# 64-row score products in pairs, the router's bias added by TensorE and its two largest read from PSUM, in a fused cross-attention and mixture-of-experts layer

## The chip, the cores and the metric

The kernel runs on one core of a Trainium2 chip. The metric is the device time of one execution in microseconds (us), and lower is better. The time shown for the kernel before is a median of three runs; the profile comes from one further execution, whose time stands beside its span below.

## The reference

What is computed, cut to what matters here (32 batches of 64 tokens, 128 features, 16 heads of 8 features, 16 experts of 64 hidden features, two experts for each token):

```python
qh, kh, vh = split_heads(layernorm(x), Wq), split_heads(ctx, Wk), split_heads(ctx, Wv)
scores = jnp.einsum('bhqd,bhkd->bhqk', qh, kh) / scale        # scale = dk ** -0.5
scores = jnp.where(mask, NEG_INF, scores)
attn = jax.nn.softmax(scores, axis=-1)
x = x + (einsum(attn, vh) joined over heads) @ Wo.T

flat = layernorm(x)
logits = flat @ router_w.T
topk_scores, topk_idx = jax.lax.top_k(logits + router_bias, 2)
topk_scores = jax.nn.softmax(topk_scores, axis=-1)            # weights of the two experts
hidden = silu(flat @ gate_e) * (flat @ up_e)                  # for each of the 16 experts
x = x + sum over experts of weight_e * (hidden @ down_e) + shared expert
```

## The kernel before, in words

Tokens are cut into 16 tiles of 128 (two batches of 64 each). The program has three stages. In the set-up, four groups of four tiles pass through `project` (lines 872 to 908): values, transposes of the normalised tokens, masked contexts, and then the queries and keys (line 903), whose heads of eight features end up on partitions. In the attention loop (`step`, lines 936 to 1003 on TensorE, with a `step` of the same numbering on each other engine) every round `t` works on several tiles at once: scores and softmax of tile `t+1`, transposes and values of tile `t`, the output projection of tile `t-1`, the second norm and the router of tile `t-2`, and on VectorE the two largest logits of tile `t-3`. In the last stage (`gate`, `up`, `down`, `slot`) the experts run as long chains of 512-column products.

Each engine has its instructions in a fixed, hand-written order and waits for semaphores that the others raise; nothing is reordered by a planner. An engine that waits holds up all that stands behind the wait.

TensorE's order in a round, as far as the change touches it: `scores(0)` (eight heads, one product over 128 rows with 512 columns, line 964); `values_as_rows` (914); four transposes of the first half of the probabilities (945); `scores(1)` (964 again, the other eight heads); `attention_transposed` (919, which waits for VectorE's attention result); four transposes of the second half (945); `norm_transposed` (930); `output_projection` (924); `values` (954, 16 small products on 32-column tiles of the array); `router` (934). A product in 32-bit floats shows in the trace as two matmul instructions.

The operands of a score product are built by GpSimd: `q_block` (418) spreads the queries so that the two batches do not mix, and `k_blocks` (426) makes, for each half of the heads, 512 columns of keys masked by head.

VectorE's order in a round: the residual add (705); the router's bias added to the logits (708); `bn_stats` (713); the largest eight (717); `bn_aggr` (721); their indices (725); the difference of the two largest (727); the negated mean (730); the indices as floats (733); `row_max(0)` (738); the reciprocal (747) and the product (749) that make the attention result of tile `t-1`; the subtraction of the maximum (759) for the first half; `row_max(1)` and the subtraction for the second half. ScalarE copies transposed probabilities (542, twice), normalises (554), copies the transposed attention result (558), copies the transposed norm twice (564, 565) and takes the exponentials (547).

From round 12 on VectorE has added work for the experts' weights (`top_two`, `two_weights`, `weigh_experts`), and from round 15 on TensorE's place for the scores is taken by the first expert products (1013).

Of the kernel before, what the change touches and what calls it, by code (L numbers as in the profile page):

```python
# [22 lines left out]
ROWS = HG * DK  # L23
# [17 lines left out]
def build_program(nc, x, ctx_nat, ctx_t, mask_row, mask_col, w_att, router_bias, w_moe, consts, out):  # L41
    stack = ExitStack()
    with stack:
# [7 lines left out]
        consts_sb = sb("consts_sb", [P, P + HG + 2 + EXPERTS])  # L51
        ident_sb = consts_sb[:, 0:P]
        hmask_sb = consts_sb[:, P:P + HG]
        half_mask_sb = consts_sb[:, P + HG:P + HG + 2]
        iota_sb = consts_sb[:, P + HG + 2:]
        bias_sb = sb("bias_sb", [P, EXPERTS])
        w_att_sb = sb("w_att_sb", [P, 4 * D + EXPERTS])
        wq_sb, wk_sb, wv_sb, wo_sb = (w_att_sb[:, i * D:(i + 1) * D] for i in range(4))
        wr_sb = w_att_sb[:, 4 * D:]
# [20 lines left out]
        half_sb = sb("half_sb", [P, P])  # L80
# [20 lines left out]
        k_blk = [sb(f"k_blk{p}", [P, 2, HG, S]) for p in range(2)]  # L101
# [10 lines left out]
        neg_mean2 = [sb(f"neg_mean2_{p}", [P, 1]) for p in range(2)]  # L112
# [5 lines left out]
        logit = [sb(f"logit{p}", [P, EXPERTS]) for p in range(2)]  # L118
        top_v = [sb(f"top_v{p}", [P, 8]) for p in range(2)]
        top_i = [sb(f"top_i{p}", [P, 8], U32) for p in range(2)]  # L120
# [78 lines left out]
        s_nmean2 = sem("s_nmean2")  # L199
# [8 lines left out]
        s_logit_sb = sem("s_logit_sb")  # L208
# [41 lines left out]
        up_ps = [banks[6], banks[0]]  # L250
        ct_ps = [banks[2][:, (2 + h) * P:(3 + h) * P] for h in range(2)]
# [133 lines left out]
        def _(pool):  # L385
            nc.gpsimd.memset(half_sb[:, :], 0.5).then_inc(s_half, 1)
# [27 lines left out]
            def q_block(t, p, first):  # L414
                if not first:
                    pool.wait_ge(s_score[1], t - 1)

                nc.gpsimd.tensor_tensor(
                    q_blk[p][:, :, :, :],
                    q_all[:, bass.ds(t, 1), :, :].rearrange("p o g (c s) -> p (o g) c s", c=1).broadcast_to([P, 2, BPT, S]),  # L420
                    half_mask_sb.rearrange("p (o b e) -> p o b e", o=1, e=1).broadcast_to([P, 2, BPT, S]), ALU.mult)

            def k_blocks(t, p):

                for g in range(2):
                    last = nc.gpsimd.tensor_tensor(  # L426
                        k_blk[p][:, g, :, :],
                        k_all[:, bass.ds(t, 1), g, :].broadcast_to([P, HG, S]),
                        hmask_sb.rearrange("p (h o) -> p h o", o=1).broadcast_to([P, HG, S]), ALU.mult)
                last.then_inc(s_blk, 1)  # L430
# [27 lines left out]
            def step(t, p, on):  # L458
                if on(-2):
                    q_block(t + 2, p, first=False)  # L460
                if on(2):
# [6 lines left out]
                    pool.wait_ge(s_nmean2, t - 1)  # L468
                    nc.gpsimd.tensor_tensor(bias2[p][:, :], neg_mean2[p][:, :], rstd2[p][:, :], ALU.mult).then_inc(s_bias2, 1)
# [19 lines left out]
        def _(act):  # L489
# [3 lines left out]
            act.dma_start(bias_sb[:, :], router_bias.broadcast_to([P, EXPERTS])).then_inc(s_wproj, 16)  # L493
# [82 lines left out]
            def tanh_of(half):  # L576

                tiles = slice(half * TILES // 2, (half + 1) * TILES // 2)
                act.wait_ge(s_top_f, (half + 1) * TILES // 2)
# [53 lines left out]
        def _(dve):  # L633
# [28 lines left out]
            nc.vector.tensor_scalar(n_valid[:, :], count_ps[:, 0:BATCHES], 1.0, None, ALU.max).then_inc(s_cnt, 1)  # L662
# [19 lines left out]
            def top_two(half):  # L682
# [4 lines left out]
                dve.wait_ge(s_top_f, (half + 1) * TILES // 2)  # L687
# [12 lines left out]
            def step(t, p, on):  # L700
# [13 lines left out]
                if on(3):  # L714
                    dve.wait_ge(s_logit_sb, t - 2)
                    nc.vector.memset(pause[:, q:q + 1], 0.0)
                    nc.vector.max(top_v[q][:, :], logit[q][:, :]).then_inc(s_top_v, 1)
# [4 lines left out]
                if on(3):  # L722
                    dve.wait_ge(s_top_v, t - 2)
                    nc.vector.memset(pause[:, 2 + q:3 + q], 0.0)
                    nc.vector.max_index(top_i[q][:, :], top_v[q][:, :], logit[q][:, :]).then_inc(s_top_i, 1)
                    tile = bass.ds(t - 3, 1)
                    nc.vector.tensor_tensor(gap[:, tile], top_v[q][:, 1:2], top_v[q][:, 0:1], ALU.subtract)
                if on(2):
                    dve.wait_ge(s_mv2, t - 1)
                    nc.vector.tensor_scalar(neg_mean2[p][:, :], mv2[p][:, 0:1], -1.0, None, ALU.mult).then_inc(s_nmean2, 1)  # L730
                if on(3):
                    dve.wait_ge(s_top_i, t - 2)
                    nc.vector.tensor_copy(top_f[:, tile, :].rearrange("p o k -> p (o k)"),
                                          top_i[q][:, 0:2]).then_inc(s_top_f, 1)
# [58 lines left out]
            dve.wait_ge(s_wproj, 32)  # L793
# [64 lines left out]
        def _(pe):  # L858
            def keep_busy(products):

                for _ in range(products):
                    nc.tensor.matmul(score_ps[0][:, 0:P], half_sb[:, :], half_sb[:, :], start=True, stop=True)
# [4 lines left out]
            nc.tensor.matmul(count_ps[:, 0:BATCHES], half_sb[:, :], valid_key[:, :], start=True,  # L867
# [4 lines left out]
            def project(g, p, first=False):  # L872
                if first:
                    pe.wait_ge(s_wproj, 32)
# [21 lines left out]
                for w, src, have, dst, drained, made in ((wq_sb, xt_sb, s_xt_sb, q_ps, s_q_sb, s_q),  # L896
# [4 lines left out]
                    for hg in range(2):  # L901
# [244 lines left out]
```

## Time and profile before

| | before |
|---|---|
| median of three runs | 193.76 us (193.52 to 194.12) |
| the profiled execution, its own time | 194.68 us |
| its span, first to last instruction | 192.9 us |
| mean granted TensorE clock | 0.976 of full speed |
| busy: TensorE, VectorE, ScalarE, GpSimd | 179.3, 168.8, 124.6, 92.1 us |
| score products, line 964 | 64 instructions, 34.0 us busy |
| key blocks, line 426 | 32 instructions, 32.7 us busy |

The page is read as follows. "Busy" of TensorE is the union of its matmuls, whose ends are modelled and reach about 0.16 us past the moment at which the next one may start; two starts therefore tell more than a duration. Weight loads (PEld) run beside the matmuls. A group "x2" in a timeline is two instructions merged into one row. An idle time in brackets names what ended it.

### The profile page before, as it was taken

To read this page: it belongs to the slowest core of one execution; us is meant where nothing else is said; L and a number is where in the kernel's file an instruction comes from. 1 tells how busy PE (TensorE), PEld (TensorE's weight loads), DVE (VectorE), ACT (ScalarE), POOL (GpSimd) and SP (SyncE) were. 2 spreads that over 40 slices of the span, in tenths; PEclk is the share of its full clock that TensorE was granted. 3 is DMA by queue.
4 is the path that set the end of the run, shared out by engine and by line. 5 is a ranking of instruction groups with operands and counts; after the bars stand their busy time and mean duration, and the time that the engine had idled before them with its cause. 6 is when DMAs were issued, how large, how long until landed. Compare 5 with 4: busy or idle time off the path is not lost.

```text
span 192.9 us, 4173 instructions
## 1 busy us (share of the span) xinstructions
PE 179.3 (93%) x1351; PEld 131.8 (68%) x1351; DVE 168.8 (87%) x515; ACT 124.6 (65%) x280; POOL 92.1 (48%) x148
## 2 busy tenths in 40 slices
PE   7599599999999999999998799999999999999962
PEld 7497467566666666666666466778888888888841
DVE  6899999589999999989995799988899889988981
ACT  2168374777888888888885855466655665565641
POOL 5746992758988988888786690300000000000000
PEclk9969979999999999999999999999999999999997
DMA  5984910000000000000000174332363236324401
GB/s 135 286 249 92 352 40 0 5 0 0 3 2 5 0 3 0 3 0 2 5 0 3 57 198 139 110 110 82 128 180 115 72 126 171 120 82 126 120 0 54
DMA packets 13202, 15.33 MB, mean 79 GB/s; under 512 B 1665, under 2 KB 8193, under 8 KB 13057
## 3 DMA queue, kind: packets, MB, share of 16 engines
q1 hardware_dynamic: 12608, 14.57, 24.8%
q10 hardware_dynamic: 576, 0.55, 1.2%
q8 instruction: 9, 0.15, 0.3%
q14 instruction: 9, 0.07, 0.1%
HBM read 13.93 MB, written 1.18 MB: 78 GB/s over the span
## 4 chain that ended last, share of the span: by engine, by line
PE 61%; DVE 19%; ACT 5%; issue 5%; POOL 0%; DVEq 0%; POOLq 0%
PE bank L1013 26%; PE bank L964 12%; PE bank L945 5%; PE bank L954 5%; DVE hid L823 2%; PE bank L903 2%; ACT hid_hi L598 2%; PE bank L934 2%; DVE prob L759 2%; PE bank L924 2%; DVE smax L738 2%; DVE xn L649 2%; DVE hid_lo L815 2%; DVE cmix_sb L823 2%; PE bank L893 1%
## 5 line engine op out<-in xcount | busy, mean ns | idle before, releaser
L589 ACT ACTIVATE sig<-bank 128x512 f32<-128x512 f32 x36 | 21.5, 600 | 21.0 <-PE bank L1013 20.4
L964 PE MATMUL bank<-k_blk,q_blk 128*128 128x512 f32 x64 | 34.0, 615 | 0.0
L426 POOL TENSOR_TENSOR k_blk<-k_all,consts_sb 128x512 f32<-128x512 f32 x32 | 32.7, 1045 | 0.0
L1013 PE MATMUL bank<-xt_hi,w_hi 128*128 (+1 forms) x72 | 29.1, 405 | 0.0
L1013 PE MATMUL bank<-xt_lo,w_hi 128*128 (+1 forms) x72 | 28.4, 394 | 0.0
L1013 PE MATMUL bank<-xt_hi,w_lo 128*128 (+1 forms) x72 | 28.3, 393 | 0.0
L542 ACT COPY prob_t<-bank 128x512 f32<-128x512 f32 x32 | 18.8, 586 | 11.5 <-PE bank L945 11.5
L806 DVE TENSOR_TENSOR hid_u<-sig,bank 128x512 f32<-128x512 f32 x32 | 21.9, 684 | 4.2 <-PE bank L1013 2.5
L738 DVE TENSOR_REDUCE smax<-bank 128x8 f32<-128x512 f32 x32 | 21.9, 686 | 2.6 <-PE bank L964 2.6
L759 DVE TENSOR_TENSOR prob<-bank,smax 128x512 f32<-128x512 f32 x32 | 22.0, 687 | 0.6
L547 ACT ACTIVATE prob<-prob 128x512 f32<-128x512 f32 x32 | 20.8, 653 | 0.0
L945 PE MATMUL bank<-consts_sb,prob 128*128 128x128 f32 x128 | 19.2, 273 | 0.0
L598 ACT CAST hid_hi<-hid 128x512 fp32r<-128x512 f32 x24 | 14.9, 621 | 6.4 <-DVE hid L823 6.4
L815 DVE TENSOR_TENSOR hid_lo<-hid,hid_hi 128x512 fp32r<-128x512 f32 x24 | 16.7, 697 | 1.7 <-ACT hid_hi L598 1.0
L1013 PE MATMUL bank<-hid_hi,w_hi 128*128 128x512 f32 (+1 forms) x37 | 15.1, 409 | 2.2 <-DVE hid_lo L815 2.2
L945 PEld LDWEIGHTS bank<-consts_sb,prob 128*128 128x128 f32 x128 | 15.1, 141 | 1.1 <-issue 1.1
L1013 PEld LDWEIGHTS bank<-xt_hi,w_lo 128*128 128x128 f32 x72 | 13.5, 188 | 3.0
L1013 PEld LDWEIGHTS bank<-xt_hi,w_hi 128*128 128x128 f32 x72 | 13.6, 189 | 2.8
L1013 PEld LDWEIGHTS bank<-xt_lo,w_hi 128*128 128x128 f32 x72 | 13.6, 188 | 2.7
L1013 PE MATMUL bank<-hid_hi,w_lo 128*128 128x512 f32 (+1 forms) x37 | 14.4, 390 | 0.0
L1013 PE MATMUL bank<-hid_lo,w_hi 128*128 128x512 f32 (+1 forms) x37 | 14.4, 388 | 0.0
L823 DVE TENSOR_TENSOR hid<-hid_u,mix_all 128x512 f32<-128x512 f32 x20 | 13.9, 697 | 0.0
(116 smaller groups left out, 378.8 us busy)
## 6 DMA issues: line engine op xcount, KB each, us to landing
mix_all<-w_rows SPq DMA_DIRECT2D x64, 128.0 KB, 2.9
w_moe_sb<-w_moe SPq DMA_DIRECT2D x1, 1728.0 KB, 9.9
x_sb<-x SPq DMA_DIRECT2D x4, 256.0 KB, 7.6
ctxt_sb<-ctx_t SPq DMA_DIRECT2D x4, 256.0 KB, 5.9
ctx_sb<-ctx_nat SPq DMA_DIRECT2D x4, 256.0 KB, 5.1
out<-x_sb SPq DMA_DIRECT2D x3, 256.0 KB, 2.3
w_att_sb<-w_att ACTq DMA_DIRECT2D x1, 264.0 KB, 5.8
mrow<-mask_row ACTq DMA_DIRECT2D x1, 256.0 KB, 4.9
```

Of the source, the lines that this page charges most:

```text
L426: last = nc.gpsimd.tensor_tensor(k_blk[p][:, g, :, :], k_all[:, bass.ds(t, 1), g, :].broadcast_to([P, HG, S]), hmask_sb.rearrange("p (h o) ...
L542: nc.scalar.copy(prob_t[p][:, h * GT:(h + 1) * GT, :], pt_ps[h][:, :].rearrange("p (j q) -> p j q", q=P)).then_inc(s_pt_sb[h], 1)
L547: nc.scalar.activation(prob[q][:, g * GN:(g + 1) * GN], prob[q][:, g * GN:(g + 1) * GN], ACT.Exp, scale=SCORE_SCALE).then_inc(s_exp[g], 1)
L589: nc.scalar.activation(sig[r][:, :], gate_ps[r][:, :], ACT.Silu).then_inc(s_sig, 1)
L738: nc.vector.tensor_reduce(smax[q][:, g * HG:(g + 1) * HG], score_ps[g][:, :].rearrange("p (h s) -> p h s", s=S), AX_X, ALU.max).then_inc(s ...
L759: nc.vector.tensor_tensor(prob[q][:, g * GN:(g + 1) * GN].rearrange("p (h s) -> p h s", s=S), score_ps[g][:, :].rearrange("p (h s) -> p h ...
L806: nc.vector.tensor_tensor(dst[:, :], sig[r][:, :], up_ps[r][:, :], ALU.mult).then_inc(s_hid_u, 1)
L815: nc.vector.tensor_tensor(hid_lo[k][:, cols], hid[k][:, cols], hid_hi[k][:, cols].bitcast(F32), ALU.subtract).then_inc(s_hid_lo, 1)
L823: nc.vector.tensor_tensor(hid[m % 3][:, :], hid_u[r][:, :], spread[k], ALU.mult).then_inc(s_hid, 1)
L945: last = nc.tensor.transpose(pt_ps[h][:, j * P:(j + 1) * P], prob[p][:, c:c + P], ident_sb)
L964: nc.tensor.matmul(score_ps[g][:, :], q_blk[q][:, g, :, :].rearrange("p b s -> p (b s)"), k_blk[q][:, g, :, :].rearrange("p h s -> p (h s) ...
L1013: last = nc.tensor.matmul(out, w, moving, start=start and k == 0, stop=stop and k == 2)
```

## The change

The score product of eight heads over 128 rows and 512 columns becomes two products of four heads each, over 64 rows and 256 columns. The rows of the two head groups lie on different halves of the array (rows 0 to 63 and 64 to 127), and their results in different PSUM banks, so a product of one group stands next to one of the other. All four products stand at the head of the round, and the second group's wait for VectorE's subtraction stands there too. The query and key projections write eight pieces of 32 partitions instead of four of 64. GpSimd builds the keys of a tile in one instruction of 512 columns instead of two.

The router's bias is now a product of its own (a matrix of ones by a row of biases) that accumulates with the logits, in columns of a PSUM bank of their own. VectorE takes the largest eight and their indices straight from PSUM. The difference of the two largest and the conversion of the indices are done once for four tiles. The negated mean is gone (GpSimd multiplies by -1 in the instruction that makes the norm's bias). The transposed norm now waits for the indices of the tile before it, where it waited for the biased logits. The DMA that spread the router's bias over the partitions is gone; the biases come with the attention weights. The matrix of halves in the set-up is one of ones, and the count is halved by VectorE.

```diff
 def k_blocks(t, p):
-    for g in range(2):
-        last = nc.gpsimd.tensor_tensor(k_blk[p][:, g, :, :], ...)
-    last.then_inc(s_blk, 1)
+    nc.gpsimd.tensor_tensor(k_blk[p][:, :, :, :], ...).then_inc(s_blk, 1)
...
-                    pool.wait_ge(s_nmean2, t - 1)
-                    nc.gpsimd.tensor_tensor(bias2[p][:, :], neg_mean2[p][:, :], rstd2[p][:, :], ALU.mult).then_inc(s_bias2, 1)
+                    nc.gpsimd.tensor_scalar(bias2[p][:, :], mv2[p][:, 0:1], rstd2[p][:, :], -1.0, ALU.mult,
+                                            ALU.mult).then_inc(s_bias2, 1)
...
-            act.dma_start(bias_sb[:, :], router_bias.broadcast_to([P, EXPERTS])).then_inc(s_wproj, 16)
...
                 if on(3):
                     dve.wait_ge(s_logit, t - 2)
-                    nc.vector.tensor_tensor(logit[q][:, :], tail_ps[:, 0:EXPERTS], bias_sb[:, :],
-                                            ALU.add).then_inc(s_logit_sb, 1)
+                    nc.vector.max(top_v[:, t - 3, :], logit_ps).then_inc(s_top_v, 1)
                 if on(2):
                     (bn_stats)
                 if on(3):
-                    dve.wait_ge(s_logit_sb, t - 2)
-                    nc.vector.max(top_v[q][:, :], logit[q][:, :]).then_inc(s_top_v, 1)
+                    dve.wait_ge(s_top_v, t - 2)
+                    nc.vector.max_index(top_i[:, t - 3, :], top_v[:, t - 3, :], logit_ps).then_inc(s_top_i, 1)
                 if on(2):
                     (bn_aggr)
-                if on(3):
-                    dve.wait_ge(s_top_v, t - 2)
-                    nc.vector.max_index(top_i[q][:, :], top_v[q][:, :], logit[q][:, :]).then_inc(s_top_i, 1)
-                    nc.vector.tensor_tensor(gap[:, tile], top_v[q][:, 1:2], top_v[q][:, 0:1], ALU.subtract)
-                if on(2):
-                    nc.vector.tensor_scalar(neg_mean2[p][:, :], mv2[p][:, 0:1], -1.0, None, ALU.mult).then_inc(s_nmean2, 1)
-                if on(3):
+                if on(3) and (t - 2) % GT == 0:
+                    nc.vector.tensor_tensor(gap[:, tiles], top_v[:, tiles, 1], top_v[:, tiles, 0], ALU.subtract)
                     dve.wait_ge(s_top_i, t - 2)
-                    nc.vector.tensor_copy(top_f[:, tile, :]..., top_i[q][:, 0:2]).then_inc(s_top_f, 1)
+                    nc.vector.tensor_copy(top_f[:, tiles, :], top_i[:, tiles, 0:2]).then_inc(s_top_f, 1)
...
-                    for hg in range(2):
-                        for b in range(BPT):
-                            last = nc.tensor.matmul(
-                                dst[b * ROWS:(b + 1) * ROWS, hg * GT * S:(hg + 1) * GT * S], ...)
+                    for j in range(2):
+                        for hg in range(2):
+                            for b in range(BPT):
+                                row, head = hg * ROWS + b * QROWS, hg * HG + j * HQ
+                                last = nc.tensor.matmul(
+                                    dst[row:row + QROWS, j * GT * S:(j + 1) * GT * S], w[:, head * DK:(head + HQ) * DK],
+                                    ..., start=True, stop=True, tile_position=(0, row))
...
             def norm_transposed(t, p):
-                    pe.wait_ge(s_logit_sb, t)
+                    pe.wait_ge(s_top_i, t)
             def router(t, p):
                 pe.wait_ge(s_xt2_hi, t + 1)
-                nc.tensor.matmul(tail_ps[:, 0:EXPERTS], xt2[p][:, :], wr_sb, start=True, stop=True).then_inc(s_logit, 1)
+                nc.tensor.matmul(logit_ps, ones_sb[:, :], bias_row_sb, start=True, stop=False)
+                nc.tensor.matmul(logit_ps, xt2[p][:, :], wr_sb, start=False, stop=True).then_inc(s_logit, 1)
...
-                def scores(g):
-                    if not (once and t < 0):
-                        pe.wait_ge(s_sub[g], t + 1)
-                    nc.tensor.matmul(score_ps[g][:, :], q_blk[q][:, g, :, :]..., k_blk[q][:, g, :, :]...,
-                                     start=True, stop=True).then_inc(s_score[g], 1)
+                def scores():
+                    for j in range(2):
+                        for g in range(2):
+                            if j == 0 and not (once and t < 0):
+                                pe.wait_ge(s_sub[g], t + 1)
+                            rows = slice(g * ROWS, (g + 1) * ROWS)
+                            last = nc.tensor.matmul(score_ps[g][:, j * HQ * S:(j + 1) * HQ * S],
+                                                    q_blk[q][rows, j, :, :]..., k_blk[q][rows, j, :, :]...,
+                                                    start=True, stop=True, tile_position=(g * ROWS, 0))
+                            if j == 1:
+                                last.then_inc(s_score[g], 1)
                 if on(-1):
                     pe.wait_ge(s_blk, t + 2)
-                    scores(0)
+                    scores()
...
                 if on(0):
                     transposes(0)
-                if on(-1):
-                    scores(1)
-                else:
+                if not on(-1):
```

## Rows read from the trace of the kernel before

**Rows 1.** Busy time by stretch: window, length, busy time of each engine, granted clock.
```profile
56.00:64.00 8.00, 8.00 (x102) 5.36 (x100) 7.65 (x35) 6.56 (x19) 7.03 (x14) 1.00 0.01 3
```

**Rows 2.** Timeline of TensorE (start us, us, engine, line): starts of rounds 2, 13, 15.
```profile
41.91 0.70 PE L964 MATMUL bank<-k_blk,q_blk 128*128 128x512 f32 x1
...
90.98 0.68 PE L964 MATMUL bank<-k_blk,q_blk 128*128 128x512 f32 x1
...
100.28 0.48 PE L1013 MATMUL bank<-xt_hi,w_hi 128*128 128x512 f32 x1
```

**Rows 3.** Timeline of TensorE in round 6.
```profile
59.77 1.10 PE L964 MATMUL bank<-k_blk,q_blk 128*128 128x512 f32 x2
60.71 0.38 PE L914 MATMUL bank<-consts_sb,pvt_sb 128*128 128x128 f32 x2
60.93 0.60 PE L945 MATMUL bank<-consts_sb,prob 128*128 128x128 f32 x4
61.37 1.02 PE L964 MATMUL bank<-k_blk,q_blk 128*128 128x512 f32 x2
62.23 0.27 PE L919 MATMUL bank<-consts_sb,att 128*128 128x128 f32 x1
62.34 0.60 PE L945 MATMUL bank<-consts_sb,prob 128*128 128x128 f32 x4
...
63.27 0.78 PE L954 MATMUL bank<-prob_t,v_all 128*18 128x64 f32 x32
63.98 0.40 PE L934 MATMUL bank<-w_att_sb,xt 128*128 128x16 f32 x2
```

**Rows 4.** Timeline of VectorE in the same round.
```profile
60.65 0.14 DVE L727 TENSOR_TENSOR gap<-top_v 128x1 f32<-128x1 f32 x1
...
60.91 0.69 DVE L738 TENSOR_REDUCE smax<-bank 128x8 f32<-128x512 f32 x1
...
61.80 0.29 DVE L749 TENSOR_TENSOR att<-bank,inv_den 128x128 f32<-128x128 f32 x1
...
63.32 0.69 DVE L759 TENSOR_TENSOR prob<-bank,smax 128x512 f32<-128x512 f32 x1
...
64.42 0.17 DVE L708 TENSOR_TENSOR logit<-bank,bias_sb 128x16 f32<-128x16 f32 x1 [0.21 <-PE bank L934]
```

**Rows 5.** Timeline of ScalarE in the same round.
```profile
61.57 0.59 ACT L542 COPY prob_t<-bank 128x512 f32<-128x512 f32 x1 [0.55 <-PE bank L945]
...
62.54 0.27 ACT L558 COPY att_t<-bank 128x128 f32<-128x128 f32 x1
62.97 0.59 ACT L542 COPY prob_t<-bank 128x512 f32<-128x512 f32 x1 [0.17 <-PE bank L945]
...
63.61 0.28 ACT L565 CAST xt_hi<-bank 128x128 fp32r<-128x128 f32 x1
```

**Rows 6.** Timeline of TensorE in the set-up; first row: a window of 0.05 us.
```profile
31.89 0.44 PE L903 MATMUL bank<-xt_sb,w_att_sb 128*64 128x256 f32 x2
...
31.89 1.08 PE L903 MATMUL bank<-xt_sb,w_att_sb 128*64 128x256 f32 x8
32.81 1.03 PE L903 MATMUL bank<-cmix_sb,w_att_sb 128*64 128x256 f32 x8
33.77 0.70 PE L964 MATMUL bank<-k_blk,q_blk 128*128 128x512 f32 x1
...
27.76 1.98 PE L964 MATMUL bank<-k_blk,q_blk 128*128 128x512 f32 x4
29.58 0.27 PE L879 MATMUL bank<-w_att_sb,ctxt_sb 128*128 128x128 f32 x1
```

**Rows 7.** Timelines of VectorE and TensorE where VectorE is late, rounds 13 and 15.
```profile
93.34 0.29 DVE L749 TENSOR_TENSOR att<-bank,inv_den 128x128 f32<-128x128 f32 x1
...
93.86 0.27 PE L945 MATMUL bank<-consts_sb,prob 128*128 128x128 f32 x1
...
103.38 0.33 PE L919 MATMUL bank<-consts_sb,att 128*128 128x128 f32 x1 [0.80 <-DVE att L749]
```

More of the change, by code:

```diff
@@ L22 @@
 HG = HEADS // 2
-ROWS = HG * DK
+HQ = HG // 2
+QROWS = HQ * DK
+ROWS = BPT * QROWS
 PAIRS = HEADS // 2
@@ L38, with build_program @@
 SCORE_SCALE = float(DK) ** 0.5
-def build_program(nc, x, ctx_nat, ctx_t, mask_row, mask_col, w_att, router_bias, w_moe, consts, out):
+def build_program(nc, x, ctx_nat, ctx_t, mask_row, mask_col, w_att, w_moe, consts, out):
     stack = ExitStack()
@@ L48, in sem @@
             return stack.enter_context(nc.semaphore(name))
-        consts_sb = sb("consts_sb", [P, P + HG + 2 + EXPERTS])
+        consts_sb = sb("consts_sb", [P, P + HQ + 2 * BPT + EXPERTS])
         ident_sb = consts_sb[:, 0:P]
[L53 to L57, printed above, removed]
+        hmask_sb = consts_sb[:, P:P + HQ]
+        half_mask_sb = consts_sb[:, P + HQ:P + HQ + BPT]
+        batch_mask_sb = consts_sb[:, P + HQ + BPT:P + HQ + 2 * BPT]
+        iota_sb = consts_sb[:, P + HQ + 2 * BPT:]
+        w_att_sb = sb("w_att_sb", [P, 4 * D + 2 * EXPERTS])
         wq_sb, wk_sb, wv_sb, wo_sb = (w_att_sb[:, i * D:(i + 1) * D] for i in range(4))
-        wr_sb = w_att_sb[:, 4 * D:]
+        wr_sb, bias_row_sb = (w_att_sb[:, 4 * D + i * EXPERTS:4 * D + (i + 1) * EXPERTS] for i in range(2))
         w_moe_sb = sb("w_moe_sb", [P, W_MOE])
@@ L100, in build_program @@
         q_blk = [sb(f"q_blk{p}", [P, 2, BPT, S]) for p in range(2)]
-        k_blk = [sb(f"k_blk{p}", [P, 2, HG, S]) for p in range(2)]
+        k_blk = [sb(f"k_blk{p}", [P, 2, HQ, S]) for p in range(2)]
         pvt_sb = sb("pvt_sb", [P, 2 * P])
@@ L116, in build_program @@
         xt2 = [sb(f"xt2_{p}", [P, P]) for p in range(2)]
-        logit = [sb(f"logit{p}", [P, EXPERTS]) for p in range(2)]
-        top_v = [sb(f"top_v{p}", [P, 8]) for p in range(2)]
-        top_i = [sb(f"top_i{p}", [P, 8], U32) for p in range(2)]
+        top_v = sb("top_v", [P, TILES, 8])
+        top_i = sb("top_i", [P, TILES, 8], U32)
         top_f = sb("top_f", [P, TILES, 2])
@@ L861, in keep_busy @@
                 for _ in range(products):
-                    nc.tensor.matmul(score_ps[0][:, 0:P], half_sb[:, :], half_sb[:, :], start=True, stop=True)
+                    nc.tensor.matmul(score_ps[0][:, 0:P], ones_sb[:, :], ones_sb[:, :], start=True, stop=True)
             pe.wait_ge(s_half, 1)
@@ L866, in _ @@
             pe.wait_ge(s_valid, 1)
-            nc.tensor.matmul(count_ps[:, 0:BATCHES], half_sb[:, :], valid_key[:, :], start=True,
+            nc.tensor.matmul(count_ps[:, 0:BATCHES], ones_sb[:, :], valid_key[:, :], start=True,
                              stop=True).then_inc(s_nvalid, 1)
@@ L900, in project @@
                         pe.wait_ge(drained, g)
[L901 to L907 removed]
+                    for j in range(2):
[4 more added lines that the diff above has]
+                                    dst[row:row + QROWS, j * GT * S:(j + 1) * GT * S], w[:, head * DK:(head + HQ) * DK],
+                                    src[p][:, :].rearrange("p (t b s) -> p t b s", b=BPT, s=S)[:, :, b, :],
+                                    start=True, stop=True, tile_position=(0, row))
                     last.then_inc(made, 1)
@@ L1118, in host_layout @@
     w_moe = np.stack([gate, up, down], axis=2).reshape(P, W_MOE)
-    w_att = np.concatenate([a["L0_xattn_" + w].T for w in ("Wq", "Wk", "Wv", "Wo")] + [a["L0_ffn_router_w"].T], axis=1)
+    bias_row = np.zeros((P, EXPERTS), np.float32)
+    bias_row[0] = a["L0_ffn_router_bias"].reshape(EXPERTS)
+    w_att = np.concatenate([a["L0_xattn_" + w].T for w in ("Wq", "Wk", "Wv", "Wo")] + [a["L0_ffn_router_w"].T, bias_row], axis=1)
     ident = np.eye(P, dtype=np.float32)
-    head_of_row = (np.arange(P) % ROWS) // DK
-    head_mask = (head_of_row[:, None] == np.arange(HG)[None, :]).astype(np.float32)
+    row = np.arange(P)
+    head_mask = (row[:, None] % QROWS // DK == np.arange(HQ)[None, :]).astype(np.float32)
+    batch_mask = (row[:, None] % ROWS // QROWS == np.arange(BPT)[None, :]).astype(np.float32)
     half_mask = (np.arange(P)[:, None] // S == np.arange(2)[None, :]).astype(np.float32)
```

49 lines of the change are left out of this document (19 added, 30 removed).

## The prediction

> **What bounds the kernel now.** I read the busy time by stretch first. In the attention loop all engines look full: TensorE is busy for 8.00 of 8.00 us, VectorE 7.65, GpSimd 7.03, ScalarE 6.56, at full clock [rows 1]. By that view a change that takes work from TensorE, VectorE and GpSimd at once must win. But a busy TensorE is not a TensorE that streams, so the next view is the timeline of one round, read for what each start waits on. Round 2 begins at 41.91 and round 13 at 90.98 [rows 2]: 11 rounds of 4.46 us. One closed path has that length. The first score product starts at 59.77 [rows 3]; VectorE's first row maximum, which needs it, starts 1.14 later at 60.91; the reciprocal and the attention product follow in VectorE's order and end at 61.80 + 0.29 = 62.09, 1.18 later [rows 4]. TensorE's line 919 waits for that, and the second four transposes start at 62.34, 0.25 later [rows 3]. ScalarE copies them from 62.97, 0.63 later, after an idle 0.17 that TensorE ends, and its last copy ends at 63.61 + 0.28 [rows 5]. The router starts at 63.98, 1.01 after 62.97, and the next scores 0.25 after that [rows 3]. 1.14 + 1.18 + 0.25 + 0.63 + 1.01 + 0.25 = 4.46. The reader is to see that the second score product is on this path only as a tie: it starts at 61.37 and takes 62.23 - 61.37 = 0.86, and line 919 starts at its end [rows 3], 0.14 after the attention result, which had to be signalled in any case.
>
> **The change part by part.**
>
> *Score products.* Each is two instructions; 512 columns take 0.86, so 256 columns take 0.215 for one instruction. No 64-row product stands in the trace; the nearest are the query and key projections, which sit on two halves of the array by columns. There two instructions start within 0.05 us, and eight of 256 columns take 32.81 - 31.89 = 0.92 and 33.77 - 32.81 = 0.96 [rows 6], where 8 x 0.215 = 1.72 would be one after another. So I take pairs as overlapping: four products are eight instructions in four slots, 0.86, plus 0.10 for weights that could not be loaded ahead (0.94 - 0.86 = 0.08 of that is paid before, between 59.77 and 60.71 [rows 3]), and 0.20 until VectorE starts, as before (60.91 - 60.71). That is 1.16 against 1.14: the pair is done when one product was done before. What is saved is 0.86 of TensorE a round in the middle, and there line 919 waits for VectorE instead. Where VectorE is late already, the second four start 93.86 - (93.34 + 0.29) = 0.23 after the attention result [rows 7] against 0.25: the gain on the path is 0.02.
>
> *Going in and out of tiles.* In the 0.96 above, 0.10 is more than four slots: leaving column tiles for the whole array costs 0.10 [rows 6]. I take the same for entering 64-row tiles after the router, on the path; between 0 and 0.20 (the two transitions around line 954 are no dearer) are its ends. Leaving them again costs as much, beside VectorE's row maximum.
>
> The Trainium skill, "TensorEngine Tiling (Array Packing)", Tiling Modes, Key Properties, says that a change of tiling mode (not of tile) drains the engine. The 0.10 agrees with it; without it the sum would be 0.10 a round lower.
>
> *The router's bias.* Two instructions of 16 columns by 128 rows more, behind the same wait for the copied norm. Four instructions that each load 128 columns take 61.37 - 60.93 = 0.44 [rows 3], and the router's own two hold the next score for 0.25, so two more cost 0.22 (between 0 and 0.25), at the one point of the round where TensorE goes straight on to the next scores.
>
> *New path.* 0.10 + 1.16 + 1.18 + 0.23 + 0.63 + 1.01 + (0.25 + 0.22) = 4.78. A second branch comes level: both scores now end before the first transposes, so the first copy of probabilities starts at 0.10 + 0.10 + 0.86 + 0.10 + 0.22 + 0.44 + 0.06 (weights not loaded ahead) + 0.20 = 2.08 after the router (before: 1.80 [rows 3, 5]); the copy of the attention result stands 0.97 behind it in ScalarE's order, and from there to the router it is 1.44 less 0.10 in which line 954 waits [rows 3, 5]: 4.39, with the router 4.86. So 4.82, 0.36 a round more.
>
> *Work taken off that lies beside the path.* GpSimd loses one of two key blocks, VectorE four small instructions (60.91 - 60.65 = 0.26 for three of them [rows 4], and the logits' add). VectorE idles for 0.21 in every round until the router is done [rows 4]; its shed work makes that idle longer. The moved wait of the second group for the subtraction is covered: VectorE needs 63.32 + 0.69 - 60.91 = 3.10 from the first row maximum to the end of the last subtraction [rows 4], so that ends at 1.26 + 3.10 = 4.36, 0.4 before TensorE gets there; if that cover went, values, transposes and all behind the scores would stand still for VectorE. The wait of the transposed norm for the indices is covered by some 2 us of other work. The projections in four column tiles cost the same if four overlap: line 954 has 32 instructions on such tiles within 63.98 - 63.27 = 0.71 [rows 3], 0.022 each where 64 columns alone would take 0.054. The DMA taken off feeds the first projection, which stands well ahead of what VectorE lets through; 0, with 1 us either way for the clock in the set-up.
>
> *Ends of the loop.* The four instructions of the first tile's scores take 29.58 - 27.76 = 1.82 [rows 6] on a TensorE with nothing between; they become 0.10 + 0.86 + 0.10 = 1.06 and a little for weights, -0.7. Rounds 0 and 1 have no router and follow VectorE: +0.1. Rounds 13 and 14 together took 100.28 - 90.98 = 9.30 [rows 2], held by VectorE's added work, which now fits: 2 x 4.82 - 9.30 = +0.34. Behind them, VectorE's shed 0.3 shortens an idle of 0.80 [rows 7], and three routers with bias add up to 0.6: +0.1.
>
> *Sum.* -0.7 + 0.1 + 11 x 0.36 + 0.34 + 0.1 = +3.8. Against the profiled execution, 194.68 (span 192.9 and 1.8 around it): 198.5. The median is 0.92 below that execution, so I expect 193.76 + 3.8 = 197.6.
>
> **The rivals.**
>
> *VectorE's round (faster).* If TensorE's streaming is what sets 4.46, as its 8.00 of 8.00 says, then 0.86 off and 0.32 on would bring it under VectorE's own round: 3.10 + 0.05 + 0.96 + 0.20 = 4.31. That is 11 x -0.15, -0.7 at the start, -0.5 in rounds 13 and 14 and -0.2 behind: -3.1, 190.7. It decides if the path from the attention result to the next scores shrinks by 0.5. Against it speaks VectorE's idle 0.21 before the logits in each round, ended by the router [rows 4].
>
> *Pairs that overlap in part.* If the second pass of a product must wait for its first and holds up its neighbour, eight instructions take five slots. The first group ends as above, the second 0.22 later, and the second branch grows to 5.08: 11 x 0.62 and about 0.3 in all else, 200.9. The Trainium skill, "TensorE: Matmul & The Clock Gate", Part 3, What overlaps and what doesn't, has matmuls start and end strictly in order; taken with two passes behind each other it gives this case. The two starts within 0.05 us [rows 6] speak against it.
>
> *No overlap.* Eight slots: the second branch grows by 0.86 to 5.7, about +17: 211. Nothing in the trace shows row tiles; that is all that speaks for it.
>
> *Nothing to be measured.* If the entry is free and the bias hides in the router's wait, a round costs 0.02 to 0.1 more, which the 0.7 at the start pays: 193.2 to 194.3.
>
> **How the numbers follow.** Forecast (0.2 to 0.45 a round, 195.7 to 198.9) 0.55, partial overlap 0.10, none 0.05, nothing 0.12, VectorE's round or another gain 0.18. A difference of 0.3% is about what a measurement of this kernel can tell from none. Faster 0.18, same 0.12, slower 0.70. The range, 191.8 to 201.2, leaves out no overlap and most of the faster case.
>
> **What would show it.** Right: rounds of 4.75 to 4.9; line 919 (in its new place) with idle time ended by the attention product; four instructions for the router, some 0.47 to the next scores; VectorE idle for 0.5 or more a round, GpSimd at some 60%. The score instructions start in pairs, four slots of 0.215; starts 0.215 apart one by one would mean no overlap. Wrong: a round of 4.3 with VectorE without idle time; a round whose scores wait for the subtraction; a clock below full in the loop.

## The result, and the profile after

| | before | after |
|---|---|---|
| median of the runs made side by side | 193.82 us (193.52 to 194.12) | 196.97 us (196.84 to 197.16) |
| ratio, 95% interval | | 1.015 (1.0112 to 1.0188) |
| profiled execution, its span | 194.68, 192.9 us | 197.0, 195.2 us |
| busy: TensorE, VectorE, ScalarE, GpSimd | 179.3, 168.8, 124.6, 92.1 us | 175.2, 164.5, 123.1, 76.8 us |
| score products | 34.0 us busy | 18.9 us busy |
| key blocks | 32.7 us busy | 16.6 us busy |

Every engine has less to do and the kernel is 3.15 us slower. The busy time by stretch (window, length, busy time of TensorE, its weight loads, VectorE, ScalarE, GpSimd, then the granted clock) answers [rows 1]: no engine is full any more.

```profile
56.00:64.00 8.00, 7.08 (x106) 5.56 (x106) 7.20 (x24) 6.00 (x17) 5.00 (x10) 1.00 0.01 2
```

TensorE's timeline of after (start us, duration us, engine, line, operation, tiles, shapes, count; in brackets the idle time before and what ended it) gives the starts of rounds 2 and 13 and of the first expert product, which answer [rows 2]; then round 6, for [rows 3]; then the set-up, for [rows 6]. Line 956 is the score products, 902 the values as rows, 907 the transposed attention result, 934 the transposes of probabilities, 922 the bias and 923 the router; 866 is the work of the set-up that follows the first tile's scores.

```profile
40.46 0.48 PE L956 MATMUL bank<-k_blk,q_blk 64*128 64x256 f32 x1
...
92.91 0.49 PE L956 MATMUL bank<-k_blk,q_blk 64*128 64x256 f32 x2
...
102.35 0.49 PE L1006 MATMUL bank<-xt_hi,w_hi 128*128 128x512 f32 x1
...
59.57 1.13 PE L956 MATMUL bank<-k_blk,q_blk 64*128 64x256 f32 x8
60.64 0.44 PE L902 MATMUL bank<-consts_sb,pvt_sb 128*128 128x128 f32 x2
...
61.97 0.33 PE L907 MATMUL bank<-consts_sb,att 128*128 128x128 f32 x1 [0.46 <-DVE att L737]
62.14 0.60 PE L934 MATMUL bank<-consts_sb,prob 128*128 128x128 f32 x4
...
63.79 0.39 PE L922 MATMUL bank<-w_att_sb,ones_sb 128*128 128x16 f32 x2
64.03 0.37 PE L923 MATMUL bank<-w_att_sb,xt 128*128 128x16 f32 x2
64.33 0.49 PE L956 MATMUL bank<-k_blk,q_blk 64*128 64x256 f32 x2
...
25.93 1.14 PE L956 MATMUL bank<-k_blk,q_blk 64*128 64x256 f32 x8
27.00 1.16 PE L866 MATMUL bank<-w_att_sb,ctxt_sb 128*128 128x128 f32 x8
...
32.52 0.70 PE L956 MATMUL bank<-k_blk,q_blk 64*128 64x256 f32 x4
```

VectorE and ScalarE in the same round, for [rows 4, 5] (line 726 is the row maximum, 737 the attention product, 705 the largest eight; 539 copies transposed probabilities, 551 normalises, 555 copies the transposed attention result):

```profile
60.74 0.69 DVE L726 TENSOR_REDUCE smax<-bank 128x8 f32<-128x512 f32 x1 [0.26 <-PE bank L956]
...
61.63 0.29 DVE L737 TENSOR_TENSOR att<-bank,inv_den 128x128 f32<-128x128 f32 x1
...
64.44 0.18 DVE L705 MAX8 top_v<-bank 128x8 f32<-128x16 f32 x1 [0.41 <-PE bank L923]
```
```profile
61.55 0.59 ACT L539 COPY prob_t<-bank 128x512 f32<-128x512 f32 x1 [1.03 <-PE bank L934]
62.03 0.50 ACT L551 ACTIVATE xn<-x_sb,bias,rstd 128x128 f32<-128x128 f32 x1
62.43 0.25 ACT L555 COPY att_t<-bank 128x128 f32<-128x128 f32 x1
62.77 0.59 ACT L539 COPY prob_t<-bank 128x512 f32<-128x512 f32 x1
```

A round lasts (92.91 - 40.46) / 11 = 4.77 where it lasted 4.46. The eight score instructions are done in 60.64 - 59.57 = 1.07, where one after another they would take 8 x 0.215 = 1.72. They start in four pairs, at 59.57, 59.89, 60.11 and 60.32, the two of a pair 6 to 7 ns apart. What they freed shows as the idle 0.46 ahead of line 907, which waits for VectorE as before. From the router to the next scores it is 64.33 - 63.79 = 0.54 where it was 0.25 [rows 3]. Nearly all of the 0.31 that a round has lost lies there.

### The profile page after: what moved, and what is told of

Same layout as the page of the kernel before. It is cut to its first block, busy times and chain, and to the rows that moved or that the text cites. A ratio compares the mean times of both kernels' runs of the same rounds, so it can differ in the third digit from the quotient of the medians.

```text
span 195.2 us, 4387 instructions
## 1 busy us (share of the span) xinstructions
PE 175.2 (90%) x1511; PEld 135.0 (69%) x1511; DVE 164.5 (84%) x443; ACT 123.1 (63%) x280; POOL 76.8 (39%) x132
## 3 DMA queue, kind: packets, MB, share of 16 engines
HBM read 13.93 MB, written 1.18 MB: 77 GB/s over the span
## 4 chain that ended last, share of the span: by engine, by line
PE 55%; DVE 20%; issue 5%; ACT 3%; DMA 3%; POOL 1%; DVEq 0%; SPq 0%
PE bank L1006 26%; PE bank L956 9%; PE bank L943 5%; DVE smax L726 5%; PE bank L934 3%; DVE hid L810 2%; PE bank L912 2%; PE bank L907 2%; PE bank L922 2%; DVE att L737 2%; ACT hid_hi L595 2%; DVE xn L646 2%; DVE cmix_sb L810 2%; DMA mix_all<-w_rows 2%; PE bank L923 1%
## 5 line engine op out<-in xcount | busy, mean ns | idle before, releaser
L539 ACT COPY prob_t<-bank 128x512 f32<-128x512 f32 x32 | 18.7, 587 | 16.6 <-PE bank L934 15.5
L956 PE MATMUL bank<-k_blk,q_blk 64*128 64x256 f32 x128 | 18.9, 403 | 0.0
L424 POOL TENSOR_TENSOR k_blk<-k_all,consts_sb 128x512 f32<-128x512 f32 x16 | 16.6, 1040 | 0.0
```

What stands on the lines that cost most here:

```text
L539: nc.scalar.copy(prob_t[p][:, h * GT:(h + 1) * GT, :], pt_ps[h][:, :].rearrange("p (j q) -> p j q", q=P)).then_inc(s_pt_sb[h], 1)
L956: last = nc.tensor.matmul(score_ps[g][:, j * HQ * S:(j + 1) * HQ * S], q_blk[q][rows, j, :, :].rearrange("p b s -> p (b s)"), k_blk[q][row ...
```

## The experiments

All edits are shown against the changed kernel, but for the last two, and cut to what matters. Each ratio is to the kernel before, run in the same set; its median there was 194.2 to 194.7 us, above the 193.82 of the result, so the ratios tell more than the times.

*Each half of the change alone.* First the pairs alone: score products, projections and key blocks as in the changed kernel; router, bias, largest two, indices and negated mean as in the kernel before.

```diff
-nc.tensor.matmul(logit_ps, ones_sb[:, :], bias_row_sb, start=True, stop=False)
-nc.tensor.matmul(logit_ps, xt2[p][:, :], wr_sb, start=False, stop=True)
+nc.tensor.matmul(tail_ps[:, 0:EXPERTS], xt2[p][:, :], wr_sb, start=True, stop=True)
...
-nc.vector.max(top_v[:, t - 3, :], logit_ps)
+nc.vector.tensor_tensor(logit[q][:, :], tail_ps[:, 0:EXPERTS], bias_sb[:, :], ALU.add)
```

> The kernel before with the score products in pairs alone (64 rows, 256 columns, all four at the head of the round, key blocks in one instruction, projections in 32-partition pieces); the router, its bias and VectorE's small instructions as before. My theory, the closed path scores, row maximum, attention product, second transposes, copies, router: a round grows by the entry into 64-row tiles (0.08) and 0.03 more until the row maximum, less 0.03 at line 919, so 4.54 us against 4.46, and the start of the loop gains about 0.6; in all 193.5 to 194.5. Rival, TensorE's streaming sets the round: 0.86 of TensorE's work goes, VectorE's round of 4.3 remains, about 191.

Then the router's part alone, with two score products over 128 rows in their old places:

```diff
-scores()
+scores(0)
...
 transposes(0)
+scores(1)
```

> The kernel before with the router's part alone (bias as a product, largest two from PSUM, difference and indices per four tiles, no DMA of the bias); scores, projections and key blocks as before. My theory: the two instructions of the bias product stand on the path, 4.46 + 0.22 = 4.68 us a round, while the start of the loop comes about 1.2 earlier for want of the DMA; 195 to 196. Rival, the work taken off VectorE counts: rounds of 4.2 to 4.3, under 192. Rival, the bias product hides behind the wait for the copied norm: 4.46, about 192.5.

And the whole change with the bias added by VectorE again:

```diff
-nc.tensor.matmul(logit_ps, ones_sb[:, :], bias_row_sb, start=True, stop=False)
+nc.vector.tensor_tensor(logit[q][:, :], logit_ps, bias_sb[:, :], ALU.add)
```

> The changed kernel with one part undone: the router's bias is added by VectorE again (one instruction from PSUM into SBUF, the largest and their indices from there), the bias by a DMA of its own that TensorE does not wait for; the rest as changed. My theory: the round falls from 4.76 to 4.54 us and the time by 11 to 13 rounds of 0.22 and a little at the end, 194 to 194.7. Rival, the bias product costs nothing: 4.76 and 197; if VectorE's instructions count, a little more than that.

Measured: pairs alone 194.91 us, ratio 1.0029 (1.0008 to 1.005); router alone 197.14, 1.015 (1.0112 to 1.0189); bias by VectorE 194.6, 1.0015 (0.9995 to 1.0036). TensorE's timelines of the three, starts of rounds 2 and 13:

```profile
41.07 0.48 PE L970 MATMUL bank<-k_blk,q_blk 64*128 64x256 f32 x1
...
91.07 0.49 PE L970 MATMUL bank<-k_blk,q_blk 64*128 64x256 f32 x2
```
```profile
41.84 0.70 PE L950 MATMUL bank<-k_blk,q_blk 128*128 128x512 f32 x1
...
93.38 0.68 PE L950 MATMUL bank<-k_blk,q_blk 128*128 128x512 f32 x1
```
```profile
40.76 0.48 PE L965 MATMUL bank<-k_blk,q_blk 64*128 64x256 f32 x1
...
90.76 0.49 PE L965 MATMUL bank<-k_blk,q_blk 64*128 64x256 f32 x2
```

Rounds of 50.00 / 11 = 4.55, 51.54 / 11 = 4.69 and 4.55. So the pairs cost 0.08 a round and the bias product 0.22 to 0.23, and the two add up to the whole change, 0.31. The rival that TensorE's streaming sets the round falls with the pairs alone: the score products held TensorE for 1.07 a round instead of 0.94 + 0.86, and the round grew. Nothing else in the change touches the round: the third kernel keeps the conversions for four tiles and goes without the negated mean, and its round is that of the pairs alone. The rounds came as expected, the times not quite. The pairs alone took 0.4 more than the upper end, which is what the kernel before took more in this set (194.21 us). The router alone took 1.1 more, since it did not begin its rounds 1.2 earlier for want of one DMA (round 0 at 33.70 against 33.77 [rows 6]). The DMA is worth nothing that shows.

*Is the router's place the cause?* If scores wait for router and bias, moving these off that place should free the round until VectorE sets it. Here the router of tile t-3 runs right behind the scores, and VectorE reads its logits at the end of its round (rounds 3 to 14):

```diff
 scores()
+router(t - 3, q)
...
-router(t - 2, p)
```

> The changed kernel with the router of tile t-3 behind the scores of round t instead of the router of tile t-2 ahead of the scores of round t+1 (rounds 3 to 14), and VectorE's reading of its logits at the end of its round. My theory: the router is the last piece of the closed path, and without it TensorE's scores wait for VectorE's last subtraction, a round of 4.3 to 4.35 us, VectorE with no idle time beyond its wait for the scores; 191 to 192.5. Rival, something else than the wait in front of the router sets the round: 4.76 stays, 197.

196.5 us, 1.0104 (1.0069 to 1.0138): from round 3 on the round is 4.62 to 4.66, not 4.3 to 4.35. TensorE's timeline of one round, then ScalarE's:

```profile
73.12 1.14 PE L971 MATMUL bank<-k_blk,q_blk 64*128 64x256 f32 x8
74.18 0.40 PE L937 MATMUL bank<-w_att_sb,ones_sb 128*128 128x16 f32 x2
...
74.90 0.60 PE L949 MATMUL bank<-consts_sb,prob 128*128 128x128 f32 x4
...
77.14 0.67 PE L958 MATMUL bank<-prob_t,v_all 128*18 128x64 f32 x32
77.74 0.49 PE L971 MATMUL bank<-k_blk,q_blk 64*128 64x256 f32 x2
```
```profile
75.53 0.59 ACT L539 COPY prob_t<-bank 128x512 f32<-128x512 f32 x1 [1.08 <-PE bank L949]
...
76.41 0.25 ACT L555 COPY att_t<-bank 128x128 f32<-128x128 f32 x1
```

The router now stands ahead of the first transposes, so ScalarE's first copy starts 75.53 - 73.12 = 2.41 behind the scores (after: 61.55 - 59.57 = 1.98), its normalising and its copy of the attention result, 0.88 later, come as late, and the values, which stand behind the transposed norm and the output projection made from these, start at +4.02 (after: 63.15 - 59.57 = 3.58). The branch through ScalarE that the prediction had named took the path over. The two rounds with a conversion for four tiles last as long (4.65 and 4.64) by another path: there VectorE's conversion takes 0.54 and the row maximum waits for VectorE. Rounds 13 and 14, 4.90 and 5.56, give back 1.0 of what the others gain against after. The router has to stand in a place where TensorE idles, and after has one, the 0.46 ahead of line 907. So the same kernel with the router behind the first four transposes:

```diff
 transposes(0)
+router(t - 3, q)
 attention_transposed(t - 1, q)
```

> The changed kernel, with the router products of tile t-3 (not t-2) run in round t for rounds 3 to 14, placed behind the first four transposes of the probabilities, where TensorE idles some 0.46 us until the attention product is ready. Theory: what holds the changed kernel's round at 4.76 is that the next score product stands behind router and bias; with these 0.45 us in an idle place, and off the path behind the last sums, the closed path is VectorE's own round, 3.10 of work and a gap of 1.22 for the score product: 4.32 a round, 12 rounds, 191 to 193 us, faster than both kernels. Rival: as in the run with the router directly behind the scores, ScalarE's queue (second copy of transposed probabilities, norm, attention copy) closes the path: 4.55 to 4.65 a round, 195 to 196.5 us.

And, since the idle place exists only because of the pairs, the same move with whole score products, the router behind the second:

```diff
-scores()
+scores(0)
...
 transposes(0)
+scores(1)
+router(t - 3, q)
 attention_transposed(t - 1, q)
```

> Unpaired scores of 128 rows, as in the kernel before, with the changed router and bias, the router products of tile t-3 run in round t behind the second half of the scores. Theory: the two halves of the scores fill TensorE up to the transposes, so that the moved products delay the transposes or the attention product's transposes; 4.5 to 4.7 a round, 194.5 to 197 us, no better than the kernel before. Rival: if only the router's place mattered and not the pairs, the round would be VectorE's, 4.3 to 4.4, and the time 191 to 193.5 us.

With pairs: 194.09 us, 0.9978 (0.9952 to 1.0004). Without: 198.29 us, 1.0198 (1.0159 to 1.0236). With pairs, TensorE in round 6, then VectorE in rounds 7 and 8 and the busy time from 58 to 72:

```profile
58.46 1.23 PE L971 MATMUL bank<-k_blk,q_blk 64*128 64x256 f32 x8
...
60.33 0.29 PE L937 MATMUL bank<-w_att_sb,ones_sb 128*128 128x16 f32 x2
...
60.86 0.33 PE L920 MATMUL bank<-consts_sb,att 128*128 128x128 f32 x1
...
62.73 0.53 PE L971 MATMUL bank<-k_blk,q_blk 64*128 64x256 f32 x2
```
```profile
63.08 0.15 DVE L722 TENSOR_TENSOR gap<-top_v 128x4 f32<-128x4 f32 x1
63.20 0.53 DVE L724 CAST top_f<-top_i 128x8 f32<-128x8 uint32 x1
...
66.77 0.69 DVE L752 TENSOR_TENSOR prob<-bank,smax 128x512 f32<-128x512 f32 x1
...
68.65 0.69 DVE L731 TENSOR_REDUCE smax<-bank 128x8 f32<-128x512 f32 x1
```
```profile
58.00:72.00 14.00, 13.38 (x208) 10.80 (x204) 13.34 (x51) 11.74 (x34) 9.44 (x19) 1.00 0.01 3
```

A round lasts 62.73 - 58.46 = 4.27 (4.22 to 4.28 in nine of the twelve from round 2 on), and VectorE goes from one instruction to the next with no wait over some 0.05 us (busy 13.34 of 14.00): its last subtraction ends at 66.77 + 0.69 = 67.46, the scores of round 8 start at 67.48, and the row maximum at 68.65, where VectorE has only just done its small instructions. The round is VectorE's, as the theory had it. The time missed its 191 to 193. What lies on VectorE is now on the path: the two rounds with a conversion for four tiles (0.15 + 0.53) took 4.75 and 4.80, and rounds 13 and 14, with VectorE's first work for the experts' weights, 5.06 and 5.30 (after: 4.76 and 4.68). And this execution's round 2 began late, at 41.47. Without pairs TensorE's timeline shows the moved products pushing line 917 behind them:

```profile
61.10 1.02 PE L965 MATMUL bank<-k_blk,q_blk 128*128 128x512 f32 x2
61.97 0.29 PE L934 MATMUL bank<-w_att_sb,ones_sb 128*128 128x16 f32 x2
...
62.33 0.31 PE L917 MATMUL bank<-consts_sb,att 128*128 128x128 f32 x1
```

There the round stays at 4.63, and at 5.1 where four tiles are converted; with rounds 13 and 14 of 5.36 and 5.71 the time is over the 194.5 to 197 expected. So, with the bias as a product, pairs and place are worth something only together: the pairs make room in the middle of the round, and something on the path has to be moved into it. Not run is the router in the idle place with the bias added by VectorE; the addition (0.17 [rows 4]) would then lie on the engine that sets the round.

*How do pairs form?* The changed kernel with the instructions of the upper 64 rows queued first, then those of the lower:

```diff
-for j in range(2):
-    for g in range(2):
+for g in range(2):
+    for j in range(2):
```

> The changed kernel with the eight score instructions of a round queued group by group: the four that use the upper 64 rows first, then the four that use the lower 64, so that only the middle two neighbours are on different halves. Theory: two instructions overlap only where neighbours in the queue use different halves: about seven slots of 0.216 in place of four, some 0.65 us more a round, 5.3 to 5.5 a round, 204 to 208 us. Rival: the halves run on their own whatever the order: 4.76 a round as in the changed kernel, 197 us.

A single execution, 198.14 us. Its timeline of TensorE: a window of 0.1 us, then the eight, then what follows them.

```profile
60.29 0.49 PE L956 MATMUL bank<-k_blk,q_blk 64*128 64x256 f32 x2
...
60.29 1.14 PE L956 MATMUL bank<-k_blk,q_blk 64*128 64x256 f32 x8
61.36 0.33 PE L902 MATMUL bank<-consts_sb,pvt_sb 128*128 128x128 f32 x1
```

Two start at once (13 ns apart) and the eight take 61.36 - 60.29 = 1.07, as in after; the rounds last 4.76. The theory of neighbours falls: the order within the score products does not matter. In the trace the second of the two carries the wait for VectorE's subtraction of the second group, so it belongs to the lower rows, and TensorE started it ahead of three instructions of the upper rows that were queued before it. The execution is 1.2 us longer than the median of after, of which the set-up holds 0.7: rounds 0 and 13 start 0.70 and 0.72 later than in after (33.22 and 93.63), with a granted clock of 0.59 from 24 to 28.

*The version the runs point to.* The kernel with the router in the idle place, with the indices of four tiles converted by ScalarE one round later, where it waits for the first transposes:

```diff
+act.wait_ge(s_top_i, t - 3)
+nc.scalar.copy(top_f[:, tiles, :], top_i[:, tiles, 0:2]).then_inc(s_top_f, 1)
...
+nc.vector.tensor_tensor(gap[:, tiles], top_v[:, tiles, 1], top_v[:, tiles, 0], ALU.subtract)
 nc.vector.max_index(top_i[:, t - 3, :], top_v[:, t - 3, :], logit_ps).then_inc(s_top_i, 1)
-four_tiles()
```

(`four_tiles` is the same difference and VectorE's conversion, so the edit also moves the difference ahead of the search for the indices.)

> The kernel with the router products in TensorE's idle place, whose rounds took 4.22 to 4.28 us with VectorE busy without a gap, and 4.75 to 4.80 where four tiles' indices were converted (conversion 0.53, difference 0.15); here ScalarE converts the indices of four tiles, one round later, ahead of its first copy of transposed probabilities, where it idled 0.58. Theory: VectorE's work is what the round lasts now, so the three longer rounds fall to 4.40 and the time by 3 x 0.4 = 1.2 to 1.5 us against that kernel, to a ratio of 0.989 to 0.993 to the kernel before, some 192.5 us. Rival: ScalarE's queue, which holds the second copy, the norm and the attention copy, closes the path as soon as anything is added to it: no gain, ratio 0.996 to 1.0.

193.05 us, 0.9951 (0.9922 to 0.998): between theory and rival in time, with the theory's rounds (4.22 to 4.37, from the start of round 2 to that of 13; the two with a conversion before, 4.32 and 4.37). Its timelines of VectorE, GpSimd and TensorE show one loss at the loop's end (line 769 is the difference, 453 GpSimd's splitting of expert weights, 943 the bias, 1029 the first expert product):

```profile
97.12 0.98 DVE L769 TENSOR_TENSOR gap<-top_v 128x4 f32<-128x4 f32 x1
...
95.17 2.92 POOL L453 TENSOR_TENSOR w_lo<-w_moe_sb,w_hi 128x384 fp32r<-128x384 f32 x3
...
98.42 0.36 PE L943 MATMUL bank<-w_att_sb,ones_sb 128*128 128x16 f32 x2 [1.39 <-DVE top_i L770]
...
98.85 0.48 PE L1029 MATMUL bank<-xt_hi,w_hi 128*128 128x512 f32 x1
```

TensorE's bias product waits for the index search, and that now stands behind a difference of 0.98: round 14 took 6.20, where the kernel without this edit took 5.30. So the edit made this loss itself, by moving the difference (why it takes so long beside GpSimd's work is taken up below, with the hardware). In the next kernel the difference of round 14 was left to the step behind the loop:

```diff
-if (t - 2) % GT == 0:
+if (t - 2) % GT == 0 and t < TILES - 2:
     nc.vector.tensor_tensor(gap[:, tiles], top_v[:, tiles, 1], top_v[:, tiles, 0], ALU.subtract)
```

> The kernel with the indices converted by ScalarE, whose round 14 shows VectorE's difference of the two largest of four tiles at 0.98 us in place of 0.15 to 0.23, from 97.12 to 98.10, while GpSimd's splitting of expert weights runs from 96.12 to 98.08, and behind it the index search on which TensorE's router products wait 1.39; here that difference is left to the step behind the loop, together with the last four tiles'. 
192.54 us, 0.9896 (0.9864 to 0.9928). TensorE:

```profile
97.75 0.37 PE L944 MATMUL bank<-w_att_sb,ones_sb 128*128 128x16 f32 x2 [0.49 <-DVE top_i L771]
...
98.19 0.48 PE L1030 MATMUL bank<-xt_hi,w_hi 128*128 128x512 f32 x1
```

The wait fell from 1.39 to 0.49, and the first expert product stands 98.19 - 92.89 = 5.30 behind the start of round 14 where it stood 98.85 - 92.65 = 6.20, which is again the 5.30 of the kernel with the router in the idle place. Of these 0.9 the spans keep less (191.2 and 191.0, with a start 0.24 later), so part is given back behind; the intervals of the last two ratios overlap, so the times alone do not tell the two kernels apart. This version is 1.0% faster than the kernel before and, by the two ratios (1.015 / 0.9896), takes 2.5% less time than the changed one.

## Why the prediction was right, and where it was off

**The path.** Forecast 0.57 + 1.16 + 1.18 + 0.23 + 0.63 + 1.01 = 4.78. Measured, in the same order: 64.33 - 63.79 = 0.54; 60.74 - 59.57 = 1.17; 61.92 - 60.74 = 1.18; 62.14 - 61.92 = 0.22; 62.77 - 62.14 = 0.63; 63.79 - 62.77 = 1.02: 4.76. The reading that a busy TensorE was not the bound, and that the path runs from scores through VectorE, ScalarE and the router back to the scores, held term by term.

**The bias and the entry into tiles.** Forecast 0.22 and 0.10. The router alone gives 4.69 - 4.46 = 0.23, the pairs alone 0.09: right in both, and the bound "hidden in the router's wait" is excluded. The entry itself is somewhat less than 0.10: from the router to the scores it is 64.33 - 64.03 = 0.30 in after and 0.32 with the pairs alone, where it was 0.25. The row from which the 0.10 was read shows less too: of the two stretches in [rows 6] only the one of 0.96 has a change of tiles behind it, and the other also takes 0.92 and not 0.86.

**The second branch.** This step failed in size. The forecast took 4.82 a round because it put ScalarE's branch at 4.86. Its copy of the attention result stands 62.43 - 61.55 = 0.88 behind the first copy, not 0.97. In ScalarE's rows of before the 0.97 is not ScalarE's order alone:

```profile
62.05 0.50 ACT L554 ACTIVATE xn<-x_sb,bias,rstd 128x128 f32<-128x128 f32 x1
62.54 0.27 ACT L558 COPY att_t<-bank 128x128 f32<-128x128 f32 x1
```

From the normalising to the copy it was 0.49, and after 62.43 - 62.03 = 0.40: the copy had waited for TensorE's line 919, which ended at 62.23 + 0.27 = 62.50 [rows 3]. That wait was taken along as if it belonged to ScalarE. So the branch comes level at 4.76 instead of above it: in after the output projection still starts 62.74 - (62.43 + 0.25) = 0.06 behind the end of that copy. The price: eleven rounds cost 52.45 - 49.07 = 3.38, not 3.96. That the branch is there was right: it set the round when the router stood directly behind the scores.

**The ends.** The first tile's scores fell to 27.00 - 25.93 = 1.07, forecast 1.06. Round 2 began 1.45 earlier, not 0.6. Of this, rounds 0 and 1 gave 0.2 (7.94 against 8.14; forecast 0.1 more). Round 0 began at 32.52 against 33.77, but the eight kernels with pairs in the set-up began it between 32.52 and 33.53 (mean 32.99) and the three without between 33.21 and 33.77 (mean 33.56): 0.57 goes with the pairs (forecast 0.7), and the other 0.7 with these two executions. Rounds 13 and 14 took 102.35 - 92.91 = 9.44 against 9.30: +0.14, not +0.34. Behind them +0.23, not +0.1. The sum is -1.45 + 3.38 + 0.14 + 0.23 = +2.3 in the spans; the profiled execution of before lay 0.9 above its median and that of after at it, which makes the 3.15 of the medians where 3.8 was forecast. Without the 0.7 of the two executions the terms give 2.98. So the forecast is near for its terms and not by luck, though their errors cancel in part: too high by 0.58 in the eleven rounds, 0.30 in rounds 0 and 1 and 0.20 in 13 and 14, too low by 0.13 at the start and 0.13 behind the loop.

**The rivals.** Partial overlap and none are excluded by the four pairs of starts: the two groups run side by side to their last instructions, which start 7 ns apart. The sentence of the Trainium skill on which partial overlap rested ("TensorE: Matmul & The Clock Gate", Part 3, What overlaps and what doesn't: matmuls strictly in order) does not describe these instructions: queued group by group, two on different halves still start together (13 ns apart), the later of them ahead of three that were queued before it. VectorE's round did not come with this change, but its condition was stated rightly: once the path lost the router, the round became VectorE's, 4.22 to 4.28 (forecast 4.31).

**What was looked for.** Rounds of 4.75 to 4.9: 4.77. The transposed attention result (919, now 907) idle until VectorE's product: 0.46. VectorE idle for 0.5 or more a round: 0.26 + 0.41. GpSimd at some 60%: 5.00 of 8.00. Four pairs of starts: seen.

## What to carry to other kernels

Follow the closed path of a round before counting busy time: work taken from a place where the engine then waits is worth nothing until something that stands on the path is moved into that place. Price separately what is put between the last wait of a round and the first product of the next, since there two instructions of 16 columns cost 0.22 in each round, as much as two of the transposes of 128 columns (0.44 for four [rows 3]). When a move opens the path, look at which engine comes next, and whether its small instructions collide with another engine's.

## What the runs showed of the hardware

*Two halves of the array by rows.* Products of 64 rows in 32-bit floats, each two instructions, ran at full overlap: eight instructions of 256 columns in 1.07, four slots of 0.216 and about 0.2 around them, in either order of the queue; the two of a slot start 6 to 14 ns apart. Queued group by group, an instruction of the lower rows starts ahead of three of the upper rows.

*VectorE and GpSimd.* The conversion of four tiles' indices took 0.17 in after (first row) and 0.53 in the kernel with the router in the idle place, where it ended at 63.73, with GpSimd's query block (second row: 63.70). The difference took 0.15 in the same round and 0.98 at the loop's end of the kernel with ScalarE's conversion, where it ended at 98.10, with GpSimd's instruction (98.09). On ScalarE the conversion took 0.20 to 0.23. It is no accident of one row: in the three kernels with the router moved and the conversion on VectorE nine conversions took 0.50 to 0.54, and each ended 0.02 to 0.03 behind an instruction of GpSimd; the other three, with GpSimd idle, took 0.17, and the four of after 0.16 to 0.17.

```profile
60.31 0.17 DVE L722 CAST top_f<-top_i 128x8 f32<-128x8 uint32 x1
```
```profile
63.08 0.62 POOL L417 TENSOR_TENSOR q_blk<-q_all,consts_sb 128x256 f32<-128x256 f32 x1
```

That VectorE waits for GpSimd is read from these ends; no run changed GpSimd's work alone. The Trainium skill, "SBUF — State Buffer", Who interferes with whom, says that the two engines share a pair of ports, which one of them holds for a whole instruction, and that a cast or an operation with two SBUF inputs on VectorE can need it; the rows agree.

*The clock in the set-up.* Where TensorE falls to its lower level (1.2 of 2.4 GHz) differs between executions. In after and in the kernel before it did so at different places (granted clock after: 0.57 from 16 to 20; before: 0.69 from 8 to 12 and 0.68 from 24 to 28). In after TensorE had been busy for 2.14 us of the 4.00 ahead of that, but in the kernel with the router directly behind the scores it had been busy for 1.91 of the 4.00 from 20 to 24, and its clock stayed full from 24 to 28. What decides is open. Round 0 of one and the same set-up begins up to 1 us apart (32.52 in after, 33.53 in the kernel with the router in the idle place), and executions of one kernel lie up to 2.3 us apart (192.41 to 194.69 for the kernel with ScalarE's conversion).
